# Two mask rows under queries and keys, half-width mask matmuls, and a re-planned order in a one-core decoder layer

## The chip, the core and the metric

The program runs on one core of a Trainium2 chip. The metric is the device time of one execution in microseconds, taken as the median of several runs. The engines that matter are TensorE (PE in the rows, its weight loads PEld), VectorE (DVE), ScalarE (ACT), GpSimd (POOL) and SyncE (SP), whose queue issues nearly all DMAs.

## What is computed

The reference is one decoder layer over x of shape 4 x 256 x 128, in three sub-layers, each followed by a layer norm:

```python
# 1. latent self-attention, 16 heads, causal
attn = q_lat @ c_kv.T / sqrt(8);  attn = where(causal, attn, -inf);  y = softmax(attn) @ c_kv ...
x = layernorm(x + y)
# 2. attention over memory (512 keys) and x itself (256 keys), 16 heads of 8
mask = j_idx > i_idx + mem_len                       # causal on the 256 own keys only
out = softmax(where(mask, -inf, q @ k.T * scale)) @ v
x = layernorm(x + out @ Wout + bout)
# 3. MLP with 64 small nets of 16 hidden units
x = layernorm(x + (relu(s[..., None] * W1 + b1) * W2).sum(-1) + b2) @ Wout + bout)
```

The last line is abridged (Win and its bias make s). What matters for the change is that the own keys are masked causally: in a tile of 128 queries by 128 keys, key j is hidden from query i when j > i. The quarter "last 64 keys, first 64 queries" of such a tile is hidden whole, two quarters are cut along their diagonal, and one is open.

## The kernel before, in words

Work is cut into 8 units: units 0 to 3 are the self-attention of the four batches, units 4 to 7 the second attention of the same batches. A unit has 4 groups of 4 heads, so there are 32 steps (unit, group), numbered 0 to 31. A step has these stages:

- **S**: scores with queries on the partitions, only to find each row's maximum. Units 0 to 3 have 4 of them per step ("own", 128 x 384); units 4 to 7 have 8 over the memory (128 x 512) and then 4 own ones. VectorE reduces each (L1036 for 512 columns, L1038 for 384), and L1043 joins them.
- **shift**: GpSimd splits the maxima into three bfloat16 parts (L849 to L855), TensorE turns them (L1303, L1306), and ScalarE, or a small DMA, writes them as three more rows under the queries, so that the next scores come out with the maximum subtracted.
- **T**: scores again with keys on the partitions (L1232), followed by the exponential on ScalarE (L934) into `probs`.
- **pv**: the product with the values (L1289).

Queries and keys live in `qk[128, slot, pair, a, 256]`, where a is 0 for queries and 1 for keys. One half of 64 partitions holds one head: 3 rows for the maxima and 48 rows of split bfloat16 parts, together ROWS = 51. Partitions 51 to 63 of a half are unused. The two halves of TensorE's rows are used by two heads next to each other. `ones_under` and `zeros_under` (L695 to L701) blank a slot with memsets before its data arrive. GpSimd does this for slots 1 to 3 at the start, and for queries again when a slot is used by a later unit (`blanked`).

The causal mask of S, and of T in units 0 to 3, is added in PSUM by `mask` (from L1187; its matmul is L1199): a 64-row identity, shifted, times a table of 0 and -3e38. Its first matmul streams 2 blocks of 128 columns, the second 2 blocks of 64. T of units 4 to 7 is masked after the exponential by GpSimd (L866).

Queries and keys reach `qk` by way of DRAM: the product (L1337, L1338), three parts on ScalarE (L953), VectorE (L1053) and then VectorE for units 0 to 3 or GpSimd for units 4 to 7 (`low_parts`, L752 and L754, L1058 and L1059 or L876 and L877), the `put` DMAs (L719 to L722) and the `take` DMAs (L739). `scr_m` and `km` are the same for the memory's keys (L725 to L727, L744).

The order of all stages on all engines is computed before the program is built, by `schedule()`: it keeps a time for each engine and each PSUM bank, and picks the next stage by start time and a rank from `COST`. `LATE` gives the step before which a load-time product (`qk`, `m`, `v1`, `vm`) isn't placed. Each engine then runs its share of this one list in order. After the last S come the last T and pv stages and the MLP (`x2T`, `s`, `hid`, `g`, `mo`; L1251 is `hid`, L1399 `g`, L1405 `mo`, L1379 `wo`, L1328 `yT` and `x2T`), which ends in a chain with filler matmuls (L1133).

## Time and profile before

| | us |
|---|---|
| median of 3 runs | 261.26 |
| the three runs | 254.71, 261.5, 261.26 |
| the profiled execution, its own time | 251.84 |
| its span, first to last instruction | 249.8 |
| PE, DVE, ACT, POOL busy | 227.6, 192.3, 181.2, 109.7 |
| mean granted TensorE clock | 0.993 |

The profiled execution is shorter than any of the three timed runs. Its stages can be read off VectorE: the first S is reduced at 18.5 us, step 16 (the first over the memory) begins at 75.6 us, the last S ends at 210.2 us, and what is left is the tail. Busy time counts overlapping work once. A TensorE that is busy is not one at its peak.

### The profile page before, as it was taken

Reading aid. Unit: us, or ns where it says so; the run is one execution under the profiler, and the core shown is the slowest. Engines: PE = TensorE matmul, PEld = TensorE weight load, DVE = VectorE, ACT = ScalarE, POOL = GpSimd, SP = SyncE. Lnnn points to the kernel's source line nnn. Section 1 sums busy time; section 2 is a strip of 40 time slices with the busy share of each in tenths; the row PEclk is TensorE's granted clock in tenths of the full one; section 3 lists DMA queues with packets and bytes.
Section 4 is the critical chain, followed back from the end, with each engine's and each line's share of the span. In section 5 each row is a group of like instructions: output and inputs, shape, how many; then the busy total and the mean of one; then the engine's idle time right before and its main releaser. Section 6 shows DMA issues by size and latency. Waiting matters only on the chain.

```text
span 249.8 us, 7711 instructions
## 1 busy us (share of the span) xinstructions
PE 227.6 (91%) x2963; PEld 140.4 (56%) x2963; DVE 192.3 (77%) x424; ACT 181.2 (73%) x391; POOL 109.7 (44%) x290
## 2 busy tenths in 40 slices
PE   8998897879997989899999999999999999999971
PEld 5676675557775746455464444564454544556651
DVE  1197787966979796899999999989999976344533
ACT  3256877887988787689957966878778988894420
POOL 8924379584665166633318413315332216241321
PEclk9999999999999997999999999999999999999999
DMA  3938920479999895870004700000000000000000
GB/s 93 372 112 238 179 31 1 130 202 167 273 174 271 182 196 127 191 125 5 3 2 130 125 5 4 5 2 3 1 4 4 1 4 4 0 24 0 25 21 21
DMA packets 20536, 21.57 MB, mean 86 GB/s; under 512 B 1244, under 2 KB 18196, under 8 KB 20372
## 3 DMA queue, kind: packets, MB, share of 16 engines
q1 hardware_dynamic: 20356, 20.96, 37.1%
q8 instruction: 23, 0.38, 0.7%
q10 hardware_dynamic: 144, 0.13, 0.2%
q14 instruction: 13, 0.11, 0.2%
HBM read 11.85 MB, written 9.18 MB: 84 GB/s over the span
## 4 chain that ended last, share of the span: by engine, by line
PE 38%; DVE 26%; POOL 14%; ACT 8%; issue 6%; DMA 4%; SPq 1%; POOLq 0%; ACTq 0%; DVEq 0%
DVE pm L1036 13%; PE psum L1289 10%; DVE pm L1038 6%; PE psum L1232 6%; ACT probs L934 5%; PE psum L1133 3%; PE psum L1212 3%; DMA qk<-scr_qk 3%; DVE left L1053 2%; PE psum L1251 2%; DMA scr_qk<-spl 2%; PE psum L1199 2%; POOL rstd L895 1%; ACT spl L953 1%; POOL km L697 1%
## 5 line engine op out<-in xcount | busy, mean ns | idle before, releaser
L934 ACT ACTIVATE probs<-psum 128x512 f32<-128x512 f32 (+1 forms) x256 | 118.2, 554 | 18.3 <-PE psum L1232 13.9
L1036 DVE TENSOR_REDUCE pm<-psum 128x1 f32<-128x512 f32 x128 | 79.5, 681 | 2.7 <-PE psum L1212 2.5
L1038 DVE TENSOR_REDUCE pm<-psum 128x3 f32<-128x384 f32 x128 | 63.1, 549 | 6.2 <-PE psum L1199 5.9
L1289 PE MATMUL psum<-probs,v 128*18 128x256 f32 (+3 forms) x1024 | 61.5, 356 | 0.9 <-ACT probs L934 0.5
L1289 PEld LDWEIGHTS psum<-probs,v 128*18 128x18 f32 (+1 forms) x1024 | 26.2, 94 | 18.7 <-ACT probs L934 5.2
L1212 PE MATMUL psum<-km,qk 51*128 51x512 bf16 x128 | 35.0, 386 | 0.6 <-ACT probs L934 0.3
L1232 PE MATMUL psum<-qk,km 51*128 51x256 bf16 x256 | 33.5, 276 | 0.3
L1232 PE MATMUL psum<-qk 51*128 51x256 bf16 (+1 forms) x256 | 31.9, 246 | 1.9 <-DVE y L1080 0.9
L866 POOL TENSOR_SCALAR_AFFINE_SELECT probs<-probs 128x512 f32<-128x512 f32 x32 | 19.8, 639 | 30.4 <-ACT probs L934 30.4
L1199 PE MATMUL psum<-neg,unit_b 64*128 64x128 bf16 (+1 forms) x256 | 30.9, 242 | 0.0
L849 POOL CAST max_s<-maxima 128x8 bf16<-128x8 f32 x32 | 6.1, 191 | 53.5 <-DVE maxima L1043 53.4
L968 ACT ACTIVATE qk<-psum 3x512 bf16<-3x512 f32 x44 | 25.7, 583 | 4.1 <-PE psum L1303 3.7
L1215 PE MATMUL psum<-qk 51*128 51x256 bf16 x128 | 26.3, 268 | 1.0 <-issue 1.0
L1214 PE MATMUL psum<-qk 51*128 51x128 bf16 x128 | 22.4, 222 | 1.9 <-ACT qk L980 0.8
L1232 PEld LDWEIGHTS psum<-qk,km 51*128 51x128 bf16 x256 | 13.5, 95 | 14.9 <-ACT probs L934 4.7
L1232 PEld LDWEIGHTS psum<-qk 51*128 51x128 bf16 x256 | 13.7, 94 | 13.2 <-ACT probs L934 5.0
L1199 PEld LDWEIGHTS psum<-neg,unit_b 64*128 64x128 bf16 x256 | 19.6, 95 | 1.7 <-issue 1.2
L1199 PE MATMUL psum<-negT,unit_b 64*128 64x128 bf16 (+1 forms) x128 | 17.1, 242 | 0.0
L1212 PEld LDWEIGHTS psum<-km,qk 51*128 51x128 bf16 x128 | 10.0, 93 | 11.2 <-ACT probs L934 4.4
L1053 DVE TENSOR_TENSOR left<-psum,spl 128x512 f32<-128x512 f32 x12 | 8.2, 686 | 8.4 <-ACT spl L953 8.4
L1214 PEld LDWEIGHTS psum<-qk 51*128 51x128 bf16 x128 | 10.5, 93 | 7.3 <-ACT probs L934 1.9
L953 ACT ACTIVATE spl<-psum 128x512 bf16<-128x512 f32 x12 | 7.2, 597 | 10.1 <-PE psum L1338 9.0
(127 smaller groups left out, 335.1 us busy)
## 6 DMA issues: line engine op xcount, KB each, us to landing
qk<-scr_qk SPq DMA_DIRECT2D x14, 384.0 KB, 6.6
km<-scr_m SPq DMA_DIRECT2D x8, 384.0 KB, 8.2
scr_qk<-spl SPq DMA_DIRECT2D x7, 384.0 KB, 3.0
scr_qk<-spl SPq DMA_DIRECT2D x21, 128.0 KB, 3.1
scr_m<-spl SPq DMA_DIRECT2D x4, 384.0 KB, 3.8
ctxT_sb<-ctxT SPq DMA_DIRECT2D x1, 1024.0 KB, 6.8
scr_m<-spl SPq DMA_DIRECT2D x4, 256.0 KB, 3.8
wb_sb<-wb SPq DMA_DIRECT2D x1, 642.0 KB, 4.8
```

Source lines behind the costliest of these rows:

```text
L866: nc.gpsimd.affine_select(out=tile, in_=tile, compare_op=ALU.is_ge, fill=0.0, base=0, pattern=[[0, 2], [0, 2], [1, P]], channel_multiplier ...
L934: nc.scalar.activation(probs[:, ring % PRING, r, 0:cols], bank_of(s)[:, 0:cols], ACT.Exp, scale=SCALE).then_inc(exp_done, 1)
L968: last = nc.scalar.activation(rows, half(m, r, PARTS).rearrange("k (a t) -> k a t", a=2), ACT.Copy, scale=-1.0)
L1036: nc.vector.tensor_reduce(pm[:, place, 1 + 4 * qt:2 + 4 * qt], m, axis=AX.X, op=ALU.max).then_inc(reduced, 1)
L1038: nc.vector.tensor_reduce(pm[:, place, 2:5], own_blocks(m), axis=AX.X, op=ALU.max).then_inc(reduced, 1)
L1053: nc.vector.tensor_sub(rest, m, high).then_inc(split_left, 1)
L1199: last = nc.tensor.matmul(block, units, part.unsqueeze(1).to_broadcast([HALF, 2, part.shape[-1]]), start=False, stop=(n == 1), skip_group_ ...
L1212: return nc.tensor.matmul(m, queries[:, qt * P:(qt + 1) * P], half(km[:, u % B, p, :], r, ROWS), start=True, stop=True)
L1214: nc.tensor.matmul(m[:, 0:P], queries[:, 0:P], keys[:, 0:P], start=True, stop=False, skip_group_check=True)
L1215: nc.tensor.matmul(m[:, P:P + T], queries[:, P:T], keys, start=False, stop=False, skip_group_check=True)
L1232: last = nc.tensor.matmul(m[:, a * (T - q0):(a + 1) * (T - q0)], keys, half(qk[:, u % B, p, 0, q0:], r, ROWS), start=(a == 0 or not masked ...
L1289: last = nc.tensor.matmul(o, v[:, at:end], weights, start=(k == 0 and not second), stop=(k == len(key_tiles(t)) - 1 and second == 1), skip ...
```

## The change

Two more rows are used in each half, ROWS and ROWS + 1, for units 1 to 7 (`patterned`). Under the queries they hold -3e38 for the first 64 queries of a tile, under the keys one for the last 64 keys of a tile and zero otherwise, so that the score matmul itself masks the quarter that is hidden whole. The two mask matmuls then cover one diagonal quarter each and stream 64 columns a block. Unit 0 keeps the old mask. The patterns are built once by GpSimd in `under_queries` and `under_keys`; slots are filled by copies of them in place of memsets, also each time that queries are blanked, and slot 0's keys are filled again before unit 4 (`first_keys`). `LATE` and `COST` get other numbers, and with them the order of all stages.

```diff
 HALF = P // 2
 DATA = SLOTS * HS
 ROWS = DATA + PARTS
+
+OWN_ROWS = ROWS + 2
 ONES = 1.0019378662109375
 SCALE = float(HS) ** -0.5
 EPS = 1e-5
...
-LATE = [(("qk", 0), 0), (("qk", 1), 0), (("qk", 2), 0), (("v1", 0), 2), (("qk", 3), 4), (("v1", 1), 0), (("m", 0), 9),
-        (("vm", 0), 10), (("m", 1), 10), (("vm", 1), 14), (("m", 2), 14), (("vm", 2), 19), (("m", 3), 15),
...
+LATE = [(("qk", 0), 0), (("qk", 1), 0), (("qk", 2), 0), (("v1", 0), 2), (("qk", 3), 0), (("v1", 1), 0), (("m", 0), 9),
+        (("vm", 0), 10), (("m", 1), 10), (("vm", 1), 16), (("m", 2), 14), (("vm", 2), 19), (("m", 3), 15),
...
 def score_cols(s):
 
     if s[0] == "S":
-        return (P + T + T + P, 4) if masked_before(s) else (MEM, 1)
+        return (P + T + (T if patterned(unit(s[1])) else T + P), 4) if masked_before(s) else (MEM, 1)
     cols = 2 * (T if own_tile(s[1], s[2]) != 1 else P)
-    return (cols + T + P, 4) if masked_before(s) else (cols, 2)
+    return (cols + (T if patterned(unit(s[1])) else T + P), 4) if masked_before(s) else (cols, 2)
 
 
 def schedule():
...
         def zeros_under(engine, queries):
 
-            return engine.memset(queries.bitcast(F32), 0.0)
+
+            return engine.tensor_copy(queries.bitcast(F32), under_queries[:, :].bitcast(F32).unsqueeze(1).to_broadcast([P, PAIRS, T // 2]))
+
+        def rows_under(engine, keys):
+
+            return engine.tensor_copy(keys.bitcast(F32), under_keys[:, :].bitcast(F32).unsqueeze(1).to_broadcast([P, PAIRS, T // 2]))
 
         def send_rows(engine, t):
...
                         engine.wait_ge(*((qk_ones, 2 * n) if n < B else (blanked, n - B + 1)))
+                        if n == B:
+                            engine.wait_ge(first_keys, 1)
...
+            nc.gpsimd.memset(under_queries[:, :].bitcast(F32), 0.0).then_inc(under_ready, 1)
+            nc.gpsimd.memset(under_keys[:, :].bitcast(F32), ONES).then_inc(under_ready, 1)
+            pool.wait_ge(under_ready, 2)
+            for r in range(2):
+                for tile, fill, first, places in ((under_queries, NEG, ROWS, (0,)), (under_queries, NEG, ROWS + 1, (P,)),
+                                                  (under_keys, 0.0, ROWS, (0, P)), (under_keys, 0.0, ROWS + 1, (HALF,))):
+                    for at in places:
+                        cols = half(tile, r, HALF)[:, at:at + HALF]
+                        nc.gpsimd.affine_select(out=cols, in_=cols, compare_op=ALU.is_ge, fill=fill, base=first - 1, pattern=[[0, HALF]],
+                                                channel_multiplier=-1).then_inc(under_ready, 1)
+            pool.wait_ge(under_ready, 12)
             for u in range(1, B):
-                ones_under(nc.gpsimd, qk[:, u, :, 1, :]).then_inc(qk_ones, 1)
+                rows_under(nc.gpsimd, qk[:, u, :, 1, :]).then_inc(qk_ones, 1)
                 zeros_under(nc.gpsimd, qk[:, u, :, 0, :]).then_inc(qk_ones, 1)
             steps = 0
             for s in plan:
...
+                        if s[1] == B:
+                            rows_under(nc.gpsimd, qk[:, 0, :, 1, :]).then_inc(first_keys, 1)
                         zeros_under(nc.gpsimd, qk[:, s[1] % B, :, 0, :]).then_inc(blanked, 1)
                 elif s in ln_no:
                     n = ln_no[s]
...
-            def mask(o, r, what):
+            def mask(o, r, what, u):
 
                 rows = half(neg if what == "S" else negT, r, HALF)
                 for n in range(2):
                     units = half(unit_b, r, HALF)[:, HALF * (1 - n):HALF * (1 - n) + P]
 
 
-                    if (what == "S") == (n == 0):
+                    if patterned(u):
+                        block, part = o[:, :, HALF * n:HALF * (n + 1)], rows[:, 0:HALF] if what == "S" else rows[:, HALF:]
+                    elif (what == "S") == (n == 0):
...
-                queries, keys = (half(qk[:, u % B, p, a, :], r, ROWS) for a in range(2))
+                rows = OWN_ROWS if src == "own" and patterned(u) else ROWS
+                queries, keys = (half(qk[:, u % B, p, a, :], r, rows) for a in range(2))
...
-                return mask(own_blocks(m)[:, 0:3:2, :], r, "S")
+                return mask(own_blocks(m)[:, 0:3:2, :], r, "S", u)
...
```

The new numbers in `COST` are `p_norm` 0.0 to 0.5, `gap` 800 to 500, `pv_few` 4 to 1, `mlp_age` from never to 6000, `p_pv` 2.2 to 3.0, `p_pv_on` 3.0 to 4.0 and `p_switch` 0 to 0.3. What they do is seen in the order.

GpSimd's queue at the start, before (`qk` is filled for slots 1 to 3):

```order
L832 CAST km<-wa_sb 128x2x2x8 x12
L697 MEMSET qk 128x8x128
L701 MEMSET qk 128x8x128
L697 MEMSET qk 128x8x128
L701 MEMSET qk 128x8x128
L697 MEMSET qk 128x8x128
L701 MEMSET qk 128x8x128
```

And with the change:

```order
L846 CAST km<-wa_sb 128x2x2x8 x12
L847 MEMSET under_queries 128x128
L848 MEMSET under_keys 128x128
L855 AFFINE_SELECT under_queries<-under_queries 64x64 x2
L855 AFFINE_SELECT under_keys<-under_keys 64x64 x3
L855 AFFINE_SELECT under_queries<-under_queries 64x64 x2
L855 AFFINE_SELECT under_keys<-under_keys 64x64 x3
L713 COPY qk<-under_keys 128x8x128
L709 COPY qk<-under_queries 128x8x128
L713 COPY qk<-under_keys 128x8x128
L709 COPY qk<-under_queries 128x8x128
```

Two memsets and ten selects are new, and the six memsets are six copies (the last two are not shown).

VectorE's queue at the start, before (L1053 to L1059 are the split of one unit's queries and keys, here the third, unit 2's; the reduces are step 0):

```order
L1053 TENSOR_TENSOR left<-psum,spl 128x512
L754 CAST spl<-left 128x512
L1058 TENSOR_TENSOR spl<-left,spl 128x256
L1059 TENSOR_TENSOR spl<-left,spl 128x256
L1038 TENSOR_REDUCE pm<-psum 128x3 x4
L1043 TENSOR_REDUCE maxima<-pm 128x4x2
```

And with the change:

```order
L1085 TENSOR_TENSOR spl<-left,spl 128x256
L1086 TENSOR_TENSOR spl<-left,spl 128x256
L1080 TENSOR_TENSOR left<-psum,spl 128x512
L768 CAST spl<-left 128x512
L1085 TENSOR_TENSOR spl<-left,spl 128x256
L1086 TENSOR_TENSOR spl<-left,spl 128x256
L1065 TENSOR_REDUCE pm<-psum 128x3 x4
L1070 TENSOR_REDUCE maxima<-pm 128x4x2
```

The fourth split (unit 3), which stood in the middle of step 8, now stands ahead of step 0.

TensorE, around the first batch's MLP, before, after the last S (L1251 is its `hid`, L1399 its `g`):

```order
L1303 MATMUL psum<-ident_b,max_s 3x128 x8
L1251 MATMUL psum<-xT_sb,wb_sb 128x256 x8
L1289 MATMUL psum<-probs,v 9x256 x4
L1232 MATMUL psum<-qk 128x128 x4
L1232 MATMUL psum<-qk,km 128x256 x4
L1289 MATMUL psum<-probs,v 9x256 x4
L1399 MATMUL psum<-hid,wb_sb 32x256 x8
```

And with the change, in steps 26 to 28:

```order
L1337 MATMUL psum<-ident_b,max_s 12x128 x2
L1320 MATMUL psum<-probs,v 18x256 x12
L1320 MATMUL psum<-probs,v 9x256 x4
L1282 MATMUL psum<-xT_sb,wb_sb 128x256 x8
L1263 MATMUL psum<-qk 128x256 x4
L1242 MATMUL psum<-km,qk 128x512 x2
```

The first batch's `hid`, `g` and `mo` have moved from behind the last S into steps 28 and 29. In return `wo` of batches 1 and 2 and `yT` of batch 2 have moved from before the last S to behind it.

## Rows read from the trace of the kernel before

**Rows 1.** Page, busy time of each engine with its share of the span.

```profile
PE 227.6 (91%) x2963; PEld 140.4 (56%) x2963; DVE 192.3 (77%) x424; ACT 181.2 (73%) x391; POOL 109.7 (44%) x290
```

**Rows 2.** Windows by stage: stretch, length, busy us of each engine, clock, DMA.

```profile
0.00:18.50 18.50, 16.51 (x88) 11.95 (x89) 8.10 (x18) 6.79 (x14) 12.59 (x36) 1.00 0.57 191
18.50:75.60 57.10, 50.95 (x827) 38.46 (x825) 44.66 (x109) 45.63 (x94) 35.61 (x91) 1.00 0.74 155
75.60:107.20 31.60, 27.61 (x363) 16.92 (x364) 26.65 (x59) 24.78 (x57) 16.05 (x38) 0.95 0.86 188
107.20:210.20 103.00, 100.27 (x1337) 53.34 (x1325) 96.98 (x197) 83.76 (x185) 35.37 (x100) 1.00 0.13 26
210.20:231.00 20.80, 20.27 (x256) 11.63 (x248) 8.25 (x23) 15.33 (x33) 5.49 (x15) 1.00 0.03 7
231.00:249.80 18.80, 12.00 (x118) 8.13 (x116) 7.65 (x23) 4.89 (x11) 4.58 (x12) 0.99 0.08 22
```

**Rows 3.** Groups by form: mask matmuls of S, and a score matmul: busy us, mean ns, idle.

```profile
L1199 PE MATMUL psum<-neg,unit_b 64*128 64x256 bf16 x128 | 26.5, 271 | 0.0
L1199 PE MATMUL psum<-neg,unit_b 64*128 64x128 bf16 x128 | 21.5, 213 | 0.0
L1215 PE MATMUL psum<-qk 51*128 51x256 bf16 x128 | 26.3, 268 | 1.0 <-issue 1.0
```

**Rows 4.** Timeline of TensorE: start, us; four own S, first and next.

```profile
143.93 0.23 PE L1214 MATMUL psum<-qk 51*128 51x128 bf16 x1
...
144.61 0.38 PE L1212 MATMUL psum<-km,qk 51*128 51x512 bf16 x1
```

**Rows 5.** Timeline of VectorE at the start: casts, subtractions, the first S.

```profile
12.67 1.44 DVE L754 CAST spl<-left 128x512 bf16<-128x512 f32 x1
14.14 0.42 DVE L1058 TENSOR_TENSOR spl<-left,spl 128x256 bf16<-128x256 f32 x1
...
15.54 0.43 DVE L754 CAST spl<-left 128x512 bf16<-128x512 f32 x1
...
18.53 0.55 DVE L1038 TENSOR_REDUCE pm<-psum 128x3 f32<-128x384 f32 x1
```

**Rows 6.** Timeline of GpSimd at the start.

```profile
4.95 0.29 POOL L820 TENSOR_SCALAR_AFFINE_SELECT neg<-neg 64x128 bf16<-64x128 bf16 x1
...
12.88 0.95 POOL L701 MEMSET qk<- 128x1024 f32 x1
20.76 0.19 POOL L849 CAST max_s<-maxima 128x8 bf16<-128x8 f32 x1 [6.93 <-DVE maxima L1043]
```

**Rows 7.** Timeline of VectorE at 43.9: the cast of the fourth split.

```profile
43.88 1.25 DVE L754 CAST spl<-left 128x512 bf16<-128x512 f32 x1
```

**Rows 8.** Timeline of GpSimd at 43.0: the memset beside that cast.

```profile
43.05 1.80 POOL L697 MEMSET km<- 128x2048 f32 x1
```

**Rows 9.** Timeline of GpSimd and of SP's queue: unit 4's low parts, blanking, load.

```profile
59.87 0.61 POOL L754 CAST spl<-left 128x512 bf16<-128x512 f32 x1 [3.26 <-DVE left L1053]
...
61.79 0.95 POOL L701 MEMSET qk<- 128x1024 f32 x1
...
67.25 0.83 SPq L739 DMA_DIRECT2D qk<-scr_qk  x2
```

**Rows 10.** Page, DMA issues: KB each, median us from issue to landing.

```profile
qk<-scr_qk SPq DMA_DIRECT2D x14, 384.0 KB, 6.6
```

**Rows 11.** Timeline of TensorE: batch 0's MLP in the tail, and a wo.

```profile
203.76 0.71 PE L1379 MATMUL psum<-wb_sb,xT_sb 128*128 128x128 f32 x4
...
212.11 1.83 PE L1251 MATMUL psum<-xT_sb,wb_sb 17*128 17x256 f32 x16
...
215.53 1.07 PE L1399 MATMUL psum<-hid,wb_sb 128*32 128x256 f32 x16
...
218.06 0.44 PE L1328 MATMUL psum<-wa_sb,x_sb 128*128 128x128 f32 x2
218.34 0.61 PE L1405 MATMUL psum<-wb_sb,xT_sb 128*128 128x128 f32 x4
```

23 lines of the change are left out of this document (13 added, 10 removed).

## The prediction, written before the change was run

> **What bounds the kernel now.** I read the busy shares first. TensorE is busy 91% of the span and VectorE 77% [rows 1], which looks like a TensorE kernel. The windows by stage correct that, and they are what the rest rests on [rows 2]. In the long middle from 107.2 to 210.2 VectorE is busy 96.98 of 103.00 us and TensorE 100.27, so both are nearly full there, and VectorE's work isn't touched by the masks. From 18.5 to 75.6 VectorE is idle 57.10 - 44.66 = 12.4 us and TensorE 6.1 us: here TensorE's bursts, loads and dependencies decide. From 75.6 to 107.2 VectorE is idle 4.95 us. After the last S, from 210.2 to 231.0, TensorE is busy 20.27 of 20.80 and VectorE only 8.25: that stretch goes by TensorE and the last exponentials. From 231.0 on the last batch's chain of dependent steps runs, which the change leaves alone. Up to 18.5 VectorE's splits set the first S [rows 5]. So a TensorE saving is paid out in full only in a part of the span.
>
> **The masks.** A mask's first matmul falls from 256 to 128 streamed columns. The two forms take 271 and 213 ns [rows 3], 58 ns apart, so columns do cost. But heads sit in two halves that stream side by side. Four own S stream 4 x 768 = 3072 columns and go by in 144.61 - 143.93 = 0.68 us [rows 4], so four times 128 columns fewer are 0.68/6 = 0.113 us a step, not 4 x 58 = 0.23 us. S has this in 28 steps (units 1 to 7), T in the 12 steps of units 1 to 3, where the four T of a step lose the same 512 columns. In the stage to 75.6 that is 12 x 2 x 0.113 = 2.7 us of TensorE, in units 4 to 7 16 x 0.113 = 1.8 us. Between nothing and all of the 2.7 us comes off the path, since VectorE idles 12.4 us there; I take 2.0, nearer to all because TensorE is busy 89% of it. The two more rows (53 for 51) cost nothing: matmuls of 256 columns take 268 ns on 51 rows and 271 on 64 [rows 3].
>
> **The start.** GpSimd's queue gets longer. The last memset of `qk` starts at 12.88 and ends at 13.83 [rows 6]. Added are two small memsets, some 0.3 us together by 0.95 us for eight times the size of one; ten selects of 64 columns, where one of 128 takes 0.29 us [rows 6], so between 1.5 and 2.9 us for ten, 2.0 taken; some 0.4 us for the two waits (an estimate between the selects' 0.29 and twice that); and six copies in place of six memsets of 0.95 us. No row has a copy of 1024 words. The nearest is a cast of 512 elements in 0.61 us [rows 9], so a copy lies between 0.95 and 1.22 us. I take 1.0, which gives 0.3 us for six (bounds 0 to 1.6). Together 3.0 us, so GpSimd is through at about 16.8 (15.7 to 18.7). Its next work begins at 20.76 [rows 6], so GpSimd itself is never late. The price is on VectorE. Its cast at 12.67 took 1.44 us and ended at 14.11, while the same cast at 15.54, with GpSimd idle, took 0.43 [rows 5]; it ended 0.28 us after the last of two memsets [rows 6]. The cast at 43.88 took 1.25 us and ended 0.28 us after the memset that started at 43.05 for 1.80 [rows 7, 8]. So such a cast waits for GpSimd's whole train. With the change the train ends 3.0 us later, and so do the first split, the first `put` and the first S: **+3.0 us**. Bounds are 1.2, if the cast slips in between two copies and its followers queue again, and 4.9.
>
> The Trainium skill (SBUF — State Buffer, "shared port pair" and what follows on contention) says that the pair is an exclusive lock of one whole instruction, given to whichever starts first, and that a VectorE operation with two SBUF inputs also blocks against a GpSimd operation that reads. The first half agrees with the 1.44 us here [rows 5], though that cast waited through two memsets, not one. The second half speaks against this change: memsets read nothing, copies do. By it the two subtractions after each cast, 0.42 us each here, would wait in turn, and cast and copies would alternate. No row here has a copy beside them.
>
> The fourth split also moves ahead of the first S: one subtraction from PSUM, a cast, two subtractions. The casts of two splits end at 14.11 and 15.97 [rows 5], so a split costs VectorE 1.9 us. In the middle the same split took 0.8 us more, for its cast waited there too [rows 7]. So +1.9 at the start and -2.7 later. A later VectorE also waits less for scores in the first steps; of the 12.4 us of idleness I count 1.0 us for this, between 0 and 2.
>
> **Unit 4.** Before, GpSimd began the low parts at 59.87, blanked the queries at 61.79, and SP loaded at 67.25 [rows 9], landing 6.6 us later [rows 10]. Now the memory's first part (1.9 us by the 61.79 - 59.87 of such a group), unit 4's own (1.9), two copies (2.0) and the second memory part (1.9) stand ahead of the load, because SP's `put` of the second memory part stands before it. GpSimd then needs 7.7 us, SP some 2.4 more for that `put` and another `take`, so the load starts about 10 us after the low parts begin, against 7.4. That is 2.6 us late; between step 15 and the first memory S VectorE now has other work (the third batch's `norm` and layer norm, about 2 us). I count nothing, and 3 us if that cover fails.
>
> **Middle and tail.** Batch 0's MLP moves from the tail to steps 28 and 29. On TensorE it is 1.83 + 1.07 + 0.61 = 3.5 us [rows 11]. Back to the tail go two `wo` at 0.71 and one transpose at 0.44, 1.9 us [rows 11]. The tail's first stretch is full of TensorE [rows 2], so it shrinks by **1.6 us**. The same 1.6 us enters the middle and eats most of the 1.8 us that the masks give back there. VectorE's middle gains two `hid` and a `mo` and loses two `wo`, about nothing. From 75.6 to 107.2 the clock was 0.95 and VectorE idle 4.95 us [rows 2]; spreading two of the layer norms over later steps I count as 1.0 us, between 0 and 3. Blanking by copies (four later ones) is hidden: GpSimd was idle half the time [rows 1].
>
> **Sum.** +3.0 +1.9 -2.7 -1.0 (start and fourth split), -2.0 (masks), -1.0 (middle), -1.6 (tail) = **-3.4 us**. Against the profiled execution's 251.84 that is 248.4, 1.35% less. The three timed runs lie at 254.71, 261.26 and 261.5, above the profiled one, for a reason that no row shows. I carry the ratio to their median: 261.26 x 0.9865 = **257.7 us**. The terms' bounds give -6.5 to +0.5 on 251.84, so 254.6 to 261.8.
>
> **Rivals.**
> - *The runs' spread decides.* The three runs are 2.7% apart with one program. If the middle run of the new kernel is of the kind of 254.71, it gives 254.71 x 0.9865 = 251.3. For it: the profiled run is of that kind too. Against it: two of three weren't.
> - *The saving goes nowhere.* The middle is VectorE's, the start's hold is real, and the masks' 2.0 us and the 1.0 us of the middle are lost in waits for other things: -0.4, so 260.8.
> - *Lock by single instructions.* The start then costs 1.2 to 2.5 us instead of 3.0: alternating 0.95 us copies with casts and subtractions of 0.42 us from 12.67 on puts the end of the second split 2.5 us later, the first 1.2. That gives -3.9 to -5.2, about 256.5. It is the lock rule of the Trainium skill's page named above.
> - *Slower: unit 4's load is late.* If the hold costs its upper 4.9 us and the cover for the load fails (+3), and the middle's saved time isn't there (+3), the sum is -3.4 + 1.9 + 3 + 3 = +4.5; with the MLP's 1.6 us showing in the full middle it is +6.1, so 267.6. It decides when the first memory S waits for `qk` or `km` by over 2 us. For it: 2.6 us of lateness are counted above. Against it: the work that now stands before it.
> - *The masks save nothing.* If a mask matmul's time is set by its issue, 2.0 us fall away, 259.8. Against it are the 58 ns [rows 3].
>
> **Chances.** My forecast 0.34, the saving lost 0.20, the low kind of run 0.20, the lock by instructions 0.10, the slower case 0.10, masks without effect 0.06. A measurement of this kernel can tell about 2% from no change, that is below 256.0 or above 266.5. Faster: the low kind, and about a third of my forecast's and a third of the lock's, which the runs' own spread carries over the bound: 0.20 + 0.11 + 0.03 = 0.34. Slower: 0.10. Within 2%: 0.56. The range has to take in the forecast, the cases of no saving and most of the low kind; it leaves out the slower one and the rest of the low kind: 250.5 to 263.5.
>
> **What would show it.** The first S on VectorE at 23 to 24 instead of 18.5, with long casts (over 1 us) for the first splits, and GpSimd's train of copies ending at about 17: the start. Own scores of a step going by in 0.57 us instead of 0.68: the masks. Step 16 beginning at about 73 to 75, without a wait for a load of `qk` or `km` before it: middle of the first half and unit 4. A stretch of 37.5 to 38 us from the last S to the end instead of 39.6: the tail. About 134 us between the first memory S and the last S: the middle is VectorE's. The forecast is wrong if that stretch shrinks by more than 3 us, for then TensorE was its bound, or if the start moves by less than 2 us, for then nothing waits for GpSimd.

## The result, and the profile after

| | before | with the change |
|---|---|---|
| runs measured together, median, us | 261.26 (5 runs) | 258.43 (5 runs) |
| the runs | 252.85, 254.71, 261.26, 261.5, 261.67 | 257.67, 257.95, 258.43, 259.79, 261.61 |
| profiled execution, its span | 251.84, 249.8 | 257.67, 255.9 |
| mean granted TensorE clock | 0.993 | 0.948 |

The ratio of the runs is **1.0177, 95% interval 1.0125 to 1.0229: the change makes the kernel 1.8% slower**. It is above one although the change's median is the lower one, because it leaves out runs more than 1.5% above the fastest of their kernel; the plain means of the five runs each are 258.40 and 259.09 us, only 0.3% apart. The kernel before falls into two groups. Over all 79 runs of it beside the change and the kernels below, 43 lie at 251.4 to 256.3 us and 36 at 258.8 to 262.7. Of 74 of them the mean granted clock is known: 0.962 to 0.991 in the 41 of the lower group, 0.935 to 0.948 in the 33 of the upper. The median of 261.26, which the prediction started from, is of the upper group.

The page's rows for the kernel with the change, first the busy times, then the granted clock in 40 slices, then two groups:

```profile
PE 237.3 (93%) x2961; PEld 145.5 (57%) x2961; DVE 191.9 (75%) x422; ACT 181.7 (71%) x393; POOL 114.8 (45%) x303
...
PEclk9996559999979999999999999999979999999997
...
L1065 DVE TENSOR_REDUCE pm<-psum 128x3 f32<-128x384 f32 x128 | 63.0, 550 | 10.3 <-PE psum L1228 10.2
...
L1228 PE MATMUL psum<-neg,unit_b 64*128 64x128 bf16 (+1 forms) x256 | 28.7, 234 | 0.0
```

TensorE is busy 9.7 us longer than before [rows 1], though it streams fewer columns. TensorE ran at 1.2 GHz from 20.9 to 38.0 us (slices 4 to 6), twice more for 3.4 us, and in the last 2.9 us.

The windows show where the 6.1 us of span went. They are cut by VectorE's reductions: first S, end of step 4, of 15, of 27, of 31 (the last S), end. Columns as in [rows 2]. First before, then the change:

```profile
0.00:18.53 18.53, 16.54 (x88) 11.98 (x89) 8.13 (x18) 6.79 (x14) 12.59 (x36) 1.00 0.57 191
18.53:33.80 15.27, 13.57 (x226) 10.66 (x227) 11.23 (x26) 10.81 (x23) 6.63 (x19) 1.00 0.92 186
33.80:75.60 41.80, 37.35 (x603) 27.76 (x602) 33.40 (x83) 34.82 (x72) 28.98 (x72) 1.00 0.67 144
75.60:178.30 102.70, 96.75 (x1270) 54.29 (x1271) 93.86 (x193) 82.19 (x182) 41.13 (x108) 0.98 0.39 83
178.30:210.10 31.80, 31.03 (x426) 15.97 (x422) 29.66 (x61) 26.25 (x59) 10.20 (x30) 1.00 0.01 3
210.10:249.80 39.70, 32.37 (x371) 19.76 (x363) 16.00 (x46) 20.32 (x45) 10.16 (x27) 1.00 0.05 14
```

```profile
0.00:22.01 22.01, 19.54 (x104) 13.98 (x105) 11.55 (x23) 7.98 (x16) 16.25 (x48) 0.97 0.57 188
22.01:41.70 19.69, 19.69 (x224) 14.20 (x222) 11.16 (x26) 11.12 (x23) 6.63 (x19) 0.60 1.04 194
41.70:82.10 40.40, 36.29 (x603) 26.46 (x595) 30.87 (x78) 34.29 (x74) 31.24 (x74) 0.96 0.44 99
82.10:181.40 99.30, 95.52 (x1233) 52.75 (x1232) 92.09 (x188) 80.10 (x178) 38.05 (x100) 1.00 0.40 90
181.40:218.80 37.40, 36.57 (x460) 19.48 (x459) 31.45 (x64) 27.93 (x62) 9.52 (x28) 0.95 0.02 6
218.80:255.90 37.10, 29.65 (x352) 18.61 (x351) 14.81 (x47) 20.26 (x46) 13.08 (x34) 0.96 0.04 12
```

Row by row the change costs +3.5, +4.4, -1.4, -3.4, +5.6 and -2.6 us. The two large losses are the second row, where TensorE is busy in every microsecond at a clock of 0.60, and the fifth.

The kernel h2 below turned out to have the change's queues, so its profile is a second execution of the change, with a span of 254.6 us. With the same cuts it costs +3.5, -0.3, +2.4, -2.3, +4.1 and -2.6 us against before. The second row's loss isn't there. Of the third row, steps 5 to 11 alone take 4.0 us more than in the first execution. In h2 these are the stretches from the first S to the end of step 4, and on to the end of step 11:

```profile
22.01:37.00 14.99, 14.70 (x224) 11.33 (x222) 11.06 (x26) 10.23 (x23) 6.63 (x19) 0.85 1.04 214
37.00:65.10 28.10, 24.23 (x379) 17.83 (x372) 18.91 (x47) 21.75 (x47) 20.11 (x47) 0.88 0.20 42
```

VectorE at the start, the rows that answer to [rows 5], and below them GpSimd's first and last copy beside it ([rows 6]):

```profile
12.66 0.68 DVE L768 CAST spl<-left 128x512 bf16<-128x512 f32 x1
13.38 1.14 DVE L1085 TENSOR_TENSOR spl<-left,spl 128x256 bf16<-128x256 f32 x1
14.44 1.25 DVE L1086 TENSOR_TENSOR spl<-left,spl 128x256 bf16<-128x256 f32 x1
...
22.01 1.95 DVE L1065 TENSOR_REDUCE pm<-psum 128x3 f32<-128x384 f32 x4
```

```profile
11.04 1.04 POOL L713 COPY qk<-under_keys 128x1024 f32<-128x1024 f32 x1
...
16.54 1.23 POOL L709 COPY qk<-under_queries 128x1024 f32<-128x1024 f32 x1
```

The cast no longer waits for GpSimd's whole train (0.68 us instead of 1.44), but the subtractions behind it take 1.14 and 1.25 us instead of 0.42 [rows 5]. The two engines take turns.

The four own S of a step, as in [rows 4]:

```profile
146.66 0.23 PE L1244 MATMUL psum<-qk 53*128 53x128 bf16 x1
...
147.22 0.38 PE L1242 MATMUL psum<-km,qk 51*128 51x512 bf16 x1
```

They go by in 0.56 us instead of 0.68. The masks do what they are meant to do on TensorE.

### The profile page after: what moved, and what is told of

Same layout as the page of the kernel before. It is cut to its first block, busy times and chain, and to the rows that moved or that the text cites. A ratio compares the mean times of both kernels' runs of the same rounds, so it can differ in the third digit from the quotient of the medians.

```text
span 255.9 us, 7723 instructions
## 1 busy us (share of the span) xinstructions
PE 237.3 (93%) x2961; PEld 145.5 (57%) x2961; DVE 191.9 (75%) x422; ACT 181.7 (71%) x393; POOL 114.8 (45%) x303
## 4 chain that ended last, share of the span: by engine, by line
PE 57%; DVE 17%; ACT 12%; issue 6%; POOL 6%; POOLq 0%; ACTq 0%; DVEq 0%
PE psum L1320 14%; PE psum L1263 9%; DVE pm L1063 8%; ACT probs L961 7%; PE psum L1242 4%; PE psum L1228 4%; DVE pm L1065 4%; PE psum L1160 3%; PE psum L1245 2%; PE psum L1244 2%; ACT qk L995 2%; PE psum L1379 2%; PE psum L1282 2%; PE psum L1430 2%; DVE left L1080 2%
## 5 line engine op out<-in xcount | busy, mean ns | idle before, releaser
L1065 DVE TENSOR_REDUCE pm<-psum 128x3 f32<-128x384 f32 x128 | 63.0, 550 | 10.3 <-PE psum L1228 10.2
L1320 PE MATMUL psum<-probs,v 128*18 128x256 f32 (+3 forms) x1024 | 63.1, 357 | 1.2 <-POOL probs L891 1.1
L1242 PE MATMUL psum<-km,qk 51*128 51x512 bf16 x128 | 37.0, 384 | 0.6
L1263 PE MATMUL psum<-qk,km 51*128 51x256 bf16 x256 | 35.5, 274 | 0.5
L874 POOL CAST max_s<-maxima 128x8 bf16<-128x8 f32 x32 | 6.1, 191 | 65.4 <-DVE maxima L1070 65.2
L1263 PE MATMUL psum<-qk 53*128 53x256 bf16 (+3 forms) x256 | 31.8, 252 | 1.7 <-issue 1.1
L1228 PE MATMUL psum<-neg,unit_b 64*128 64x128 bf16 (+1 forms) x256 | 28.7, 234 | 0.0
L1245 PE MATMUL psum<-qk 53*128 53x256 bf16 (+1 forms) x128 | 27.6, 288 | 0.0
L995 ACT ACTIVATE qk<-psum 3x512 bf16<-3x512 f32 x44 | 25.7, 585 | 2.1 <-PE psum L1334 1.6
L1244 PE MATMUL psum<-qk 53*128 53x128 bf16 (+1 forms) x128 | 22.9, 232 | 2.2 <-issue 1.4
L1263 PEld LDWEIGHTS psum<-qk,km 51*128 51x128 bf16 x256 | 13.4, 94 | 15.5 <-issue 3.8
L1228 PEld LDWEIGHTS psum<-neg,unit_b 64*128 64x128 bf16 x256 | 20.6, 101 | 1.1
L1263 PEld LDWEIGHTS psum<-qk 53*128 53x128 bf16 (+1 forms) x256 | 13.9, 96 | 12.0 <-ACT probs L961 3.9
L1244 PEld LDWEIGHTS psum<-qk 53*128 53x128 bf16 (+1 forms) x128 | 10.8, 96 | 8.3 <-ACT probs L961 3.3
L1228 PE MATMUL psum<-negT,unit_b 64*128 64x128 bf16 (+1 forms) x128 | 14.6, 237 | 0.0
```

The lines of the kernel that those rows point to most:

```text
L995: last = nc.scalar.activation(rows, half(m, r, PARTS).rearrange("k (a t) -> k a t", a=2), ACT.Copy, scale=-1.0)
L1065: nc.vector.tensor_reduce(pm[:, place, 2:5], own_blocks(m), axis=AX.X, op=ALU.max).then_inc(reduced, 1)
L1228: last = nc.tensor.matmul(block, units, part.unsqueeze(1).to_broadcast([HALF, 2, part.shape[-1]]), start=False, stop=(n == 1), skip_group_ ...
L1242: return nc.tensor.matmul(m, queries[:, qt * P:(qt + 1) * P], half(km[:, u % B, p, :], r, ROWS), start=True, stop=True)
L1244: nc.tensor.matmul(m[:, 0:P], queries[:, 0:P], keys[:, 0:P], start=True, stop=False, skip_group_check=True)
L1245: nc.tensor.matmul(m[:, P:P + T], queries[:, P:T], keys, start=False, stop=False, skip_group_check=True)
```

## The experiments

"Ratio" is always against the kernel before on the same chip. Step ends and half-clock stretches (TensorE granted 1.2 GHz) are read from each kernel's one profiled execution.

**The kernel before again (g1).** No edit.

> The kernel before, run once more. Theory A (the clock of TensorE): the runs of this one program fall in two groups, those of about 253 us with a mean clock of 0.98 or more and those of about 261 us with 0.96 or less, and the missing clock lies between 20 and 38 us. Theory B (something else spreads the runs, DMA for instance): runs of 261 us show the same clock as runs of 253 us.

Ratio 0.9963 (0.9915 to 1.0012), median 253.2 us, with 3 of 10 runs at 258.2 to 261.6. Their clock was 0.936 to 0.953, that of the other seven 0.973 to 0.991. So theory A holds as to the level of the clock, and the spread belongs to the program, not to the occasion. Where the clock is missing in a slow run isn't shown, since none was profiled.

**Masks alone and order alone (g2, g3).** g2 has the new masks, rows and copies with `LATE`, `COST` and `score_cols` of before, so its order is exactly the old one. g3 has the old masks and the new order:

```diff
-LATE = [... (("qk", 3), 4), ... (("vm", 1), 14), ... (("vm", 3), 26)]
+LATE = [... (("qk", 3), 0), ... (("vm", 1), 16), ... (("vm", 3), 28)]
 and the new numbers in COST
```

> Two mask rows, narrow masks and GpSimd's copies, with the order of the kernel before kept stage for stage. If the new order is what costs, this one is at 250 to 254 us with the clock as before and a first S at 19.7 to 21 us instead of 18.5, less 2 us for the masks later. If the copies at the start are what makes the clock fall, this one falls too, with a clock of about 0.5 from 20 us on, and takes 256 to 261 us.

> The change's order with the old masks and memsets, so no copies at the start and a first S at 20.4 us (the fourth split ahead of it, 1.9 us). If the order makes the clock fall, it is about 258 to 262 us with a half clock from 20 to 38 us. If the copies do, it stays at the full level there and takes 251 to 255 us, and only the dip near 188 us is left.

g2: ratio **1.0279** (1.0168 to 1.0391), 260.75 us. g3: **1.012** (1.004 to 1.02), 256.92 us. Neither part gains alone. g2 took the time that its expectation gave to copies which make the clock fall, g3 a time between its two branches, with half-clock stretches at 15.4 to 25.7 and 39.3 to 46.1 us. g2's ratio is a high estimate: its four runs, 259.93 to 261.55 us at clocks of 0.934 to 0.941, lie where the upper group of the kernel before lies, and the plain means of that session, 260.74 and 257.03, are 1.4% apart. In g2 steps 5 to 11 took 28.34 us, before 28.33, and steps 23 to 31 took 70.39 against 70.60. The narrower masks bought nothing there. In g3 VectorE's first cast came at 10.19 us instead of 12.67, because TensorE's clock rose earlier in that execution (below, at i1). It met more of the memsets and waited for all that were left:

```profile
10.19 3.92 DVE L753 CAST spl<-left 128x512 bf16<-128x512 f32 x1
14.14 0.43 DVE L1057 TENSOR_TENSOR spl<-left,spl 128x256 bf16<-128x256 f32 x1
```

GpSimd's last memset ended there at 13.83. With memsets the wait is for the whole train, with copies it is in turns.

**TensorE kept busy at the start (g4).** 21 filler matmuls between the changed kernel's first stages.

```diff
+            FILLS = {("rep", 0): 4, ("S", 0): 3, ("rep", 3): 3, ("S", 1): 3, ("v1", 0): 3, ("rep", 5): 3, ("shift", 1): 2}
+                if s[:2] in FILLS and s[:2] not in done_fill: keep_warm(FILLS[s[:2]], heads)
```

> The changed kernel with 21 filler matmuls of zeros (128 x 256, 0.11 us each at the full level) in TensorE's queue among the first stages up to the shift of step 1. If the half clock of 20 to 38 us comes from too little work on TensorE at the start and costs 4 to 5 us, this one keeps the full level there, its step 3 ends at 33 to 35 us instead of 37.7, and it takes 251 to 254 us. If the clock there is the chip's own doing, nothing changes, or the fillers cost up to 2 us: 258 to 260.

Ratio 1.02 (1.0112 to 1.0289), 258.84 us. The half-clock stretch shrank from 17.1 us to 6.8, and step 4 ended at 36.8 instead of 41.7. But TensorE then stood still, and a second stretch came at 38.9 to 45.8. Three windows of g4:

```profile
20.00:30.00 10.00, 10.00 (x101) 6.98 (x100) 6.82 (x16) 4.54 (x9) 3.32 (x10) 0.74 1.04 237
30.00:37.00 7.00, 6.88 (x134) 5.12 (x132) 5.15 (x14) 6.11 (x16) 3.31 (x9) 1.00 1.14 166
37.00:42.00 5.00, 0.26 (x6) 0.15 (x7) 0.88 (x2) 0.84 (x2) 2.53 (x6) 0.69 0.41 62
```

```profile
41.79 0.62 PE L1326 MATMUL psum<-probs,v 128*18 128x256 f32 x5 [4.74 <-issue]
```

For 4.74 us TensorE waited for nothing that the profile shows. In the record of instruction fetches a 16 KB block was moved from 38.74 to 40.23 us, where before one was moved from 32.84 to 34.06. Whose instructions it holds isn't in the record; that it is what TensorE waited for is my reading. Until 37 us the DMA share was at 1.0 or above: with the fourth product moved ahead, six loads stand in a row (about 23 to 26 us) where four stood.

This does not show that the fillers did anything. h2, the change without them, also had a first stretch of 6.8 us, ended step 4 at 37.0, then stood still, and had a second stretch at 40.2 to 47.0:

```profile
41.55 0.26 PE L1247 MATMUL psum<-qk 53*128 53x128 bf16 x1 [3.58 <-issue]
```

What g4 gained over the change's first execution lies within what one program does from one execution to the next.

**Batch 0's MLP back to the end (h1).** `hid` is not placed while an S is left. The rest of the order is as in the change.

```diff
-                if step < LATE_STEP.get(s, 0):
+                if step < LATE_STEP.get(s, 0) or s[0] == "hid" and maxima:
```

> The changed kernel with one rule more in the planner: no hid product before the last S is placed. The order is the same, stage for stage, up to the place in step 28 where the first batch's MLP stood; the MLP is behind the last S again. In the changed kernel steps 28 and 29 took 22.9 us together, before 14.5. If the MLP and the half clock that follows it cost 3 us net, this one takes 3 us less than the changed kernel (about 255), steps 28 and 29 take about 14.5 us and the tail from the last S is 2 to 3 us longer. If the tail's saving pays for the move, it stays at 258.

Ratio 1.046 (1.0211 to 1.0708), 266.11 us, where I had expected 255 to 258. Steps 28 to 31 took 35.0 us instead of 37.4, but the tail 44.0 instead of 37.1. In this order the early MLP pays, though part of the 266.11 us is clock: this execution had half-clock stretches of 23.9, 6.8 and 6.8 us.

**Unit 3's load later (h2, i3).** h2 was meant to delay unit 3's `take`, but the edit left SyncE's queue as it was, so it measures the changed kernel once more (its profile is used above). i3 does it:

```diff
+            late = ("take", "qk", 3)
+            order.insert(order.index(("put", "m", 0)), late)
+                if s == late:
+                    sp.wait_ge(reduced, s_no[("S", 7, 0)] + 1)
```

> The changed kernel; only in SP's queue unit 3's load (2 DMAs of 384 KB) stands later, after unit 4's neighbour, the put of the memory's first part is reached (it is needed in step 12 only). If six loads in a row keep TensorE's program from being fetched, its stall for nothing seen (1.4 us at 44 in the changed kernel, 4.7 at 37 in the one with fillers, 2.6 at 37 in the order alone) is gone, and the kernel takes 1 to 3 us less. If the stalls come from elsewhere, they stay and the time is as it was.

> The changed kernel; unit 3's load waits in SP's queue until step 7 is begun, so that four loads go in a row and not six. (The earlier try set it at a place with nothing of SP's in between, and so was the changed kernel once more.) If TensorE's program fetch stands behind the loads, the fetch that landed at 38 to 41 us lands at about 35, the stall of 1.4 to 4.7 us is gone, and so is the half clock at 40 to 47: 2 to 5 us less. If not, the stall stays at its place.

h2: ratio 1.0165 (0.9932 to 1.0398), 258.31 us, the change's own time. i3: 0.9895 (0.9759 to 1.003), 254.1 us from 4 runs that spread over 250.75 to 258.05. The 16 KB block was moved from 36.17 to 37.46 us, and TensorE still waited 2.2 us for nothing that the profile shows, until 38.87. It looked like a repair, and j4 below takes that back.

**New masks for units 4 to 7 only (h3).** Units 1 to 3 keep the old masks, and the start its memsets. The patterns are built after step 2.

```diff
 def patterned(u):
-    return u > 0
+    return u >= B
```

> The changed kernel with the mask rows in units 4 to 7 only: memsets at the start as in the kernel before, the patterns built after step 2, the order the same. Units 1 to 3 have the old masks. If the copies at the start cost 1.6 us by holding VectorE, and the masks of units 1 to 3 give nothing, the first S is at 20.4 us (22.0 in the changed kernel) and the kernel takes 1.5 to 3 us less than it. If the narrow masks of units 1 to 3 do give 2 us, it is no faster.

Ratio 1.026 (1.0128 to 1.0391), 260.02 us, so the 1.5 to 3 us less than the change did not come. This is the most telling kernel. Its queues on VectorE, ScalarE and SyncE are those of g3 from end to end, TensorE's up to its 536th row, which is beyond step 15, and GpSimd's up to the patterns, which it builds from 33.4 us on. The half-clock stretch was 15.4 to 25.7 us in g3 and 14.7 to 38.6 in h3. The same stretch from the first S to the end of step 4, first in g3, then in h3:

```profile
20.40:36.50 16.10, 15.63 (x234) 11.83 (x232) 11.17 (x27) 10.90 (x24) 6.62 (x19) 0.84 1.07 232
```

```profile
20.40:42.00 21.60, 21.49 (x235) 15.29 (x234) 11.28 (x27) 11.76 (x24) 8.96 (x31) 0.58 0.93 178
```

The same engine programs ran 5.5 us longer there, at a clock of 0.58 instead of 0.84, and at 33.4 us, where GpSimd's queues part, TensorE was 3.4 us behind already. The change and h2, which have all instructions in common, had stretches of 17.1 and 6.8 us. **The length of the half-clock stretch is no function of the instructions in it.**

h3 and g3 also separate what the new masks do in units 4 to 7. Steps 12 to 15 took 16.3 us in h3 and 13.8 in g3. There GpSimd prepares unit 4: it makes low parts and, with the new masks, copies two patterns into `qk` where one memset was. The splits of the next maxima into three parts, which TensorE needs for the shift, stand behind this in its queue. In the change this group lasts from 61.88 to 69.37 us, in g3 from 60.24 to 66.64. TensorE's waits for GpSimd's maxima from 66 to 96 us, first before, then the change:

```profile
PE psum L1303 <- POOL max_s L855: 0.3, 1, 0.3
```

```profile
PE psum L1334 <- POOL max_s L880: 1.8, 2, 1.2
```

All 20 executions profiled fall on one side or the other:

| units 4 to 7 | executions | TensorE waits for the maxima, steps 12 to 15 | half clock in steps 12 to 15 | steps 12 to 15, us |
|---|---|---|---|---|
| old masks | 8 | 0.3 to 0.6 us | in none | 13.4 to 13.8, k2 14.8 |
| new masks | 12 | 1.6 to 1.8 us | in 11, for 3.4 or 6.8 us | 16.0 to 17.8, j2 14.4 |

j2 is the one without the half clock, and has the smallest loss, 0.9 us against i1.

**h1, h2 and h3 together (h4)** gave 263.93 us, ratio 1.0385 (1.0037 to 1.0732), where 250 to 255 was expected. It says nothing beyond h1 and h3.

**GpSimd held off VectorE's splits (i1, j1 on before, i2 on the change).**

```diff
             for u in range(1, B):
+                if u == 2:
+                    pool.wait_ge(split_done[split_no[("qk", 2)]], 1)
```

> The kernel before; GpSimd's four memsets for slots 2 and 3 wait for VectorE's third split (done at 18.5 us), so that none runs beside the first splits. Where TensorE's clock rises at 5 us and not at 14, VectorE reaches its first cast at 10.2, and in the order-only kernel that cast then stood 3.9 us, behind all memsets; TensorE ran dry and the clock fell. If this is what makes the slow half of the runs of the kernel before, those runs go (all runs 249 to 254 us) and the cast takes 0.43 us. If the clock falls for another cause, the runs still spread from 252 to 262.

> The changed kernel; the four copies for slots 2 and 3 wait for the third split. If the copies' hold costs 1.2 to 1.6 us at the start and helps the clock to fall, the first S comes at 20.5 to 21 us, and the kernel takes 2 to 6 us less than the changed one's 258. If the fourth split ahead of the first S is enough to make the clock fall, the half clock at the start stays and it gains 1.5 us at most.

i1: ratio **0.9934** (0.9881 to 0.9988), 251.84 us, with all ten runs at 250.48 to 256.42. i2: 1.0122 (0.9997 to 1.0246), 257.28 us. In i1 GpSimd waits, and VectorE's cast takes 0.43 us instead of 1.44:

```profile
12.66 0.43 DVE L754 CAST spl<-left 128x512 bf16<-128x512 f32 x1
...
18.19 1.95 DVE L1040 TENSOR_REDUCE pm<-psum 128x3 f32<-128x384 f32 x4 [0.59 <-PE psum L1201]
```

```profile
17.66 0.95 POOL L697 MEMSET qk<- 128x1024 f32 x1 [7.38 <-DVE spl L1061]
```

A second profiled execution of before, taken beside these (i4, 254.85 us), had no half-clock stretch before 106 us either, and neither had g1's.

The executions differ in one more thing, which the clock column of the windows doesn't show, because it counts as 1.00 what lies before the first clock record. TensorE ran slower at first. The same two matmuls, in before and in j1:

```profile
11.92 1.06 PE L1338 MATMUL psum<-xT_sb,w 128*128 128x256 f32 x2
```

```profile
9.16 0.59 PE L1340 MATMUL psum<-xT_sb,w 128*128 128x256 f32 x2
```

The first record of the full clock is at 14.05 us in before and at 5.37 in j1. Over the 20 executions it lies at 4.3 to 5.7 us in twelve, and all twelve later fell to half clock ahead of step 5. It lies at 12.9 to 14.1 in eight. Of these the four with the old order and the old masks (before, g1, i1, i4) didn't fall there, and the four with the new order and the new masks (the change, h2, i2, j4) did. An early rise brings VectorE's first cast to about 10 us, where the memsets aren't through. That the hold helps by sparing such an execution the 3.92 us of g3 fits j1, an early one with a cast of 0.43 us and 252.31 us in all, but no early execution of the kernel before itself was profiled.

**The square of masks and order with the hold (j1, j2, j3), and both repairs (j4).** j1 is i1 again, j2 is g2 with the hold, j3 is g3 with the hold, j4 is the change with the hold and i3's edit.

> The code before, with GpSimd's memsets of query and key slots 2 and 3 held until the third block of scores has been split. The same kernel as i1, whose median was 251.84 us, 0.9934 of the time before. Theory (VectorE's starts next to GpSimd's memsets are what costs at the start): 250.5 to 253.5 us, 0.985 to 0.998. Rival (the 10 runs of i1 were a good draw): no less than the time before, 253 to 256 us.

> The masks of the change (two rows under queries and keys, 64 columns a block) in the order before, with GpSimd's copies into slots 2 and 3 held until the third block is split. With i1 (neither), i2 (masks and new order) and j3 (new order) it makes a square. Theory (the masks save nothing in the old order, and their copies cost VectorE's starts): first S at 20.5 us as before, and 252 to 255 us, where the same masks without the hold took 260.75. Masks that save what was predicted (2 us in units 1 to 7): 249 to 251 us. Rival (narrow masks in themselves let TensorE's clock fall): 257 to 261 us, with half-clock stretches as in g2.

> The new order with the masks of before, GpSimd's memsets of slots 2 and 3 held until the third block is split. Theory (the order itself costs: a fourth split ahead of the first S, six loads in a row, steps 28 and 29): 254.5 to 257.5 us, i.e. no better than g3's 256.92 by more than 2, first S at about 22.4. Rival (what cost in the order was only VectorE's start beside GpSimd): 251 to 253 us.

> The changed kernel with both repairs of the start: the copies into slots 2 and 3 held, and unit 3's load of queries and keys held until step 7's first scores are reduced. Theory (both costs are real and separate): 252.5 to 255.5 us, TensorE waiting for no instruction after 38 us; the end from step 27 on stays 3 us longer than before, so it doesn't beat j1. Rival (only one of them counts, i3's 254.1 being a draw): 256 to 258.5 us. If the new order and the masks are worth what was predicted in the middle and at the end once the start is mended: 248 to 251 us.

| ratio to before (95% interval) | old masks | new masks |
|---|---|---|
| old order | 1 | g2 1.0279 (1.0168 to 1.0391) |
| old order, hold | j1 **0.9922** (0.988 to 0.9963) | j2 1.0114 (1.0062 to 1.0167) |
| new order | g3 1.012 (1.004 to 1.02) | the change 1.0177 (1.0125 to 1.0229) |
| new order, hold | j3 0.9998 (0.9948 to 1.0049) | i2 1.0122 (0.9997 to 1.0246) |

In every row the new masks are the slower column, by 0.6 to 2.8%. With the old order the intervals are apart; with the new order they overlap. The order costs 0.8 to 1.2% with the old masks, where j3's and j1's intervals overlap, and nothing or less with the new ones. j2, at 256.28 us, was slower than the 252 to 255 expected of masks that save nothing, and i2 gained about 1 us on the change where 2 to 6 was hoped for. j4 came to 1.0162 (1.0103 to 1.0222), no better than i2: **the later load is no repair**, and its expectation failed.

Where j2 loses against i1 is seen in windows. First i1, then j2, the same five cuts (first S, steps 4, 15, 27, 31):

```profile
0.00:18.19 18.19, 16.20 (x85) 11.80 (x87) 7.21 (x19) 6.79 (x14) 9.57 (x33) 1.00 0.61 205
18.19:33.20 15.01, 13.97 (x237) 10.88 (x235) 11.22 (x26) 10.92 (x23) 9.71 (x23) 1.00 0.90 177
33.20:75.00 41.80, 37.28 (x602) 27.77 (x598) 33.36 (x83) 34.80 (x72) 29.10 (x72) 1.00 0.67 146
75.00:176.60 101.60, 95.59 (x1270) 53.48 (x1270) 93.30 (x193) 81.93 (x182) 41.16 (x108) 1.00 0.38 83
176.60:208.50 31.90, 31.14 (x432) 15.98 (x422) 29.74 (x61) 26.33 (x59) 10.33 (x30) 1.00 0.01 3
```

```profile
0.00:16.29 16.29, 13.50 (x96) 9.96 (x98) 8.62 (x19) 6.74 (x14) 12.38 (x44) 0.95 0.66 219
16.29:37.60 21.31, 20.71 (x229) 15.04 (x229) 11.31 (x27) 11.72 (x23) 10.54 (x23) 0.56 0.66 132
37.60:80.30 42.70, 36.45 (x600) 27.10 (x592) 33.40 (x83) 34.76 (x72) 30.07 (x73) 1.00 0.67 144
80.30:182.20 101.90, 94.80 (x1270) 52.91 (x1270) 93.38 (x194) 81.75 (x182) 41.53 (x108) 1.00 0.39 82
182.20:213.90 31.70, 30.97 (x430) 15.82 (x418) 29.55 (x61) 26.26 (x59) 10.31 (x30) 1.00 0.01 3
```

From step 5 on, TensorE's busy time fell by 0.83, 0.79 and 0.17 us, and the stretches took 0.9, 0.3 and -0.2 us longer. TensorE was given time and idled in it. The 0.9 us lie in steps 12 to 15, as above; steps 5 to 11 took 28.4 us in both.

The first two rows can't be compared so, because the clock rose at 4.5 us in j2 and at 13.8 in i1. j1 is the one to set beside j2, with 15.14 us to the first S against 16.29, and this from there to the end of step 4:

```profile
15.14:33.20 18.06, 15.86 (x224) 12.33 (x223) 11.16 (x26) 11.41 (x23) 10.19 (x23) 0.81 0.82 157
```

So j2 loses 1.2 us up to the first S and 3.3 us more up to the end of step 4, at a clock of 0.56 instead of 0.81. In the latter stretch (steps 0 to 4) all but the last step is unit 0, with its old masks.

**The fourth product put back (k1 with the new masks, k2 with the old, both with the hold).**

```diff
-LATE = [... (("qk", 3), 0), ...
+LATE = [... (("qk", 3), 4), ...
```

> The changed kernel with the fourth load-time product of queries and keys put back to step 4, where the kernel before has it (masks and all other numbers of the new order stay), and GpSimd's copies into slots 2 and 3 held until the third block of scores is split. Against i2 (1.0122) it undoes the fourth split ahead of the first S and the row of six loads. Theory (the fourth split costs 1.9 us there, and TensorE's clock then falls): first S at 20 to 22 us, step 4 ends at 34 to 38 instead of 41, and 252.5 to 255.5 us. Rival (the fourth split is worth its place, since it leaves the middle): first S earlier by 1.9, but the stretch to step 11 longer by 2 to 3, and 256 to 259 us.

> The same without the masks: the masks of before, the new order but for the fourth product back at step 4, memsets of slots 2 and 3 held. What is left of the new order is the middle and the end (the MLP of batch 0 in steps 28 and 29, the layer norms, fewer stages in the tail). Against j1 (0.9922) it tells what that is worth: theory 0.992 to 1.002, since steps 28 to 31 took 5 us more in every kernel with the new order and the tail gives back 2.6. Rival (the new order's middle and end gain, the loss being all in the start): 0.980 to 0.990. Against k1 it tells the masks alone in this order: theory k1 is 0.5 to 1.2% longer, as with the other orders; rival: k1 is shorter by 1.4 to 2 us.

k1: ratio **1.0448** (1.0373 to 1.0522), 266.4 us; k2: **1.0368** (1.0293 to 1.0443), 263.73 us. Both expectations failed, for a reason that lies in the kernel and not on the chip: the number feeds the planner, and it made another order all the way down. In its first part k2 does show what was asked. Its first S starts at 14.99 and step 4 ends at 31.3, in j3 17.22 and 38.5; j3 gives back 2.0 us from step 5 to 11 (23.8 against 25.8 us). Step 15 ends at 71.8, 3.8 us ahead of before. Then steps 28 to 31 take 46.0 us:

```profile
177.50:223.50 46.00, 44.04 (x561) 23.49 (x560) 34.19 (x72) 34.38 (x76) 11.95 (x35) 0.95 0.05 8
```

So k1 and k2 don't measure the fourth split alone, and what the rest of the new order is worth stays unmeasured.

## Why the prediction was wrong

The time forecast for the change, 257.7 us, lay 0.7 us from its median, and that is no merit: a base of the upper group, 261.26, times a ratio of 0.9865, where the ratio was 1.0177. The sum said -3.4 us on the profiled execution, and it was +6.1 on the span, +4.8 in h2. The slower rival's sum was +6.1 too, also by luck: its parts (a hold of 4.9 us, a late load) didn't happen. The terms' bounds, added up straight, give -8.9 to +2.5; the prediction's -6.5 to +0.5 is narrower, and no working is shown for it.

- **The step that failed: from the first S to the end of step 15.** The sum took 5.7 us off this stretch (-2.7 for the fourth split, -2.0 for the masks, -1.0 for fewer waits), and counted nothing for TensorE's clock and nothing for unit 4. It took 60.1 us instead of 57.1, in h2 59.2. Step 16 was to begin at 73 to 75 us and began at 82.1. The first S, with +4.9 us forecast, moved by 3.5; the misses came behind it.
- **TensorE's clock.** From the first S to the end of step 4 the change took 4.4 us more, at a clock of 0.60, where before it was 1.00 up to step 15 [rows 2]. Across eight executions this stretch took 15.27 and 15.01 us at a clock of 1.00, 14.99 at 0.85, 16.10 at 0.84, 18.06 at 0.81, 19.69 at 0.60, 21.60 at 0.58 and 21.31 at 0.56. These are up to 6.3 us, more than any term of the sum. They don't add up with the rest: h2, with 14.99 us, lost most of the difference in the standstill that followed, and step 11 ended at 66.1 us in the change, 65.4 in h2 and 62.3 before.
- **How GpSimd holds VectorE.** The forecast had the cast wait for the whole train; measured are turns. GpSimd's train ended at 17.8 us, 3.9 later than before where 3.0 was forecast, but VectorE didn't wait for its end. Measured are also 1.14 to 1.25 us for subtractions of 0.42. The second split's last subtraction ended at about 18.4 instead of 16.8, 1.6 us later, within the 1.2 to 2.5 of the rival "lock by single instructions". The other 1.9 us of the 3.5 are the fourth split, as forecast. The Trainium skill (SBUF — State Buffer, "Who interferes with whom") says that a VectorE operation with two SBUF inputs blocks against a GpSimd operation that reads SBUF, not against one that only writes it. By it the subtractions wait beside copies and not beside memsets, and the traces agree: 1.14 and 1.25 us beside copies, 0.42 and 0.43 beside a memset in j3 (at 16.55 and 16.89 us). The same section has the lock held for one whole instruction, and that doesn't describe the cast of 3.92 us in g3, which waited through several memsets.
- **The masks, -2.0.** The size on TensorE was right, 0.56 us for four own S where 0.57 was forecast. The path's share was wrong: I argued from a TensorE that is busy 89% of that stage that nearly all of its saving comes off the path. In j2 against i1, same order, none did from step 5 on. Busy is not bound. The rival "the masks save nothing" was right that they save nothing, for the wrong reason, and missed that they cost something.
- **The fourth split leaves the middle, -2.7.** Its size isn't shown. Steps 5 to 11 took 28.3 us before, 24.1 in the change and 28.1 in h2, which is the same program; j3 and k2 took 23.8 and 25.8.
- **The middle, -1.0, and the "about 134 us" to the last S.** It took 136.7 us, before 134.5. Two parts hide in it: -3.4 us up to step 27 and +5.6 in steps 28 to 31, where TensorE was busy 36.57 of 37.40 us and VectorE only 31.45. I had let the MLP's 1.6 us vanish in what the masks give back. In that stretch TensorE was the bound (5.5 us more busy, 1.7 of them from 3.4 us at half clock), so what moved into it came out. In h2, with no half clock there, it took 35.9 us, busy 35.06. All seven executions with the old order took 31.7 to 31.8 us for these steps, all nine with the change's order 35.9 to 37.7.
- **The tail, -1.6.** -2.6 us. Right in sign, and 37.1 us against a forecast of 37.5 to 38.
- **Unit 4, counted as nothing.** The load was forecast about 10 us behind the low parts, measured are 72.18 - 61.88 = 10.3 us; steps 16 to 18 took 28.3 us against 31.5, and nothing waited for the load. What was late was something else in GpSimd's queue: the maxima behind unit 4's copies. TensorE waited 1.8 us for them instead of 0.3, its clock then fell for 3.4 us, and steps 12 to 15 took 16.2 us instead of 13.4, in h2 16.0. Of this the new masks make 2.2 to 2.5 us (h3, the change and h2 against g3).
- **The runs' spread.** Named as a rival, and its level was the right one for before (253.5 us is the median of the lower group over all its runs). The upper group has the lower clock, 0.935 to 0.948; when and why it loses it isn't shown, since none of its executions was profiled. With the hold of i1 and j1, 22 of 22 runs lie at 249.7 to 256.4 us, with nothing above, though their clocks go down to 0.947.

**What stays open.** Of what the new masks cost, the 2.2 to 2.5 us of steps 12 to 15 are shown (0.9 in j2), and 1.2 us up to the first S in j2 against j1. The rest sits in half-clock stretches between 15 and 40 us. Two executions of one program differ there by 10.3 us of half clock (the change and h2) and by 6.8 (i1 and j1), so one profiled execution per kernel can't tell a cause from chance. What starts the stretch wasn't found, nor what makes the clock rise at 5 or at 14 us. That the six loads in a row delay TensorE's instructions wasn't shown either: with the load later, i3 still waited 2.2 us, and j4, which didn't wait, was at half clock then.

**The better kernel.** The kernel before with the hold alone, j1 and i1: 0.9922 (0.988 to 0.9963) and 0.9934 (0.9881 to 0.9988). It is ahead of both kernels of this case by an edit of two lines, though by less than the 2% that a measurement here can call a difference; on plain means, with no run left out, it is 1.5 and 1.7% ahead of the kernel before.

## What to carry to other kernels

A saving on an engine that is busy 89 or 97% of a stretch is worth nothing until a wait that ends on that engine is named; look at how the stretch's length moves, not at its busy time. When work is added to a helper engine, ask what stands behind it in that engine's queue, at every place where it is added, and not only whether the engine has idle time. Before adding work to one engine's start, look for another engine's short instructions beside it that already take two or three times their usual time, and try to move the disturber first. Profile one program twice before a difference between two profiles is given a cause. And don't carry a ratio to a median before knowing whether the runs form one group or two.
